# The near part added to the square table by VectorE, and the far and square products made by GpSimd

## The reference

```
x_aff = clip(x * a + b, -1.5, 1.5);  u = (x_aff + 1) * 0.5 * (K - 1)
i = floor(u);  t = clip(u - i, 0, 1);  b0..b3 = cubic basis of t
spline = alpha[i-1]*b0 + alpha[i]*b1 + alpha[i+1]*b2 + alpha[i+2]*b3     (indices clipped to 0..K-1)
y = id_gain * x + sum over r of spline[r] * mix[c, r] + bias
```

## Time and profile before

| what | value |
|---|---|
| time, median of 3 runs | 1149.39 us (1149.33 to 1150.38) |
| span of the profiled execution, first to last instruction | 1143.4 us |
| the rest, around the span | 6.0 us, if the profiled execution took the median time |
| busy share of PE / DVE / ACT / POOL | 95% / 85% / 79% / 12% |
| spline stage | from about 416 us to the end |

### The profile page before, as it was taken

How to read it: one execution, slowest core, us unless ns; L and a number is a source line. 1 busy time by engine, 2 the same in 40 slices (tenths; PEclk the granted TensorE clock), 3 DMA queues, 4 the chain that set the end, 5 groups by cost and what they waited for, 6 DMA issues and landing times.

```text
span 1143.4 us, 51639 instructions
## 1 busy us (share of the span) xinstructions
PE 1088.0 (95%) x23882; PEld 726.6 (64%) x23882; DVE 969.9 (85%) x959; ACT 898.8 (79%) x410; POOL 138.8 (12%) x195
## 2 busy tenths in 40 slices
PE   6999999699999959999999999999999999999996
PEld 5777777577777735666666656565665666566564
DVE  4856656687767679999999999999998999999997
ACT  4445453766777548999999999999999999999971
POOL 6000000068100000110101101011010110110100
PEclk9999999899999989999999999999999999999999
DMA  8677674677676937799999999989999989999652
GB/s 278 227 293 283 251 283 175 220 257 301 248 296 270 373 137 173 183 235 232 221 228 218 222 236 216 224 201 236 226 214 231 218 217 235 219 226 209 150 127 86
DMA packets 57459, 259.37 MB, mean 227 GB/s; under 512 B 16080, under 2 KB 16080, under 8 KB 49232
## 3 DMA queue, kind: packets, MB, share of 16 engines
q1 hardware_dynamic: 48496, 208.40, 56.0%
q0 software_dynamic: 8640, 48.17, 23.1%
q10 hardware_dynamic: 160, 0.30, 0.1%
HBM read 104.29 MB, written 77.07 MB: 159 GB/s over the span
## 4 chain that ended last, share of the span: by engine, by line
PE 86%; DVE 7%; issue 3%; DMA 1%; ACT 1%; SPq 0%; ACTq 0%; DVEq 0%
PE tab L1302 48%; PE acc L741 30%; PE tab L1311 7%; DMA halo<-y_scratch 1%; DMA w_raw<-in_w 1%; DVE middle_mask L1160 1%; ACT xin L381 1%; ACT yout L420 1%; DVE far L1187 0%; DVE far_sq L1209 0%; DVE stats L547 0%; DVE lin L1139 0%; DVE offset L1153 0%; DVE edge_mask L1169 0%; DVE poly L1215 0%
## 5 line engine op out<-in xcount | busy, mean ns | idle before, releaser
L1302 PE MATMUL tab<-edge_mask,diag 128*32 128x392 bf16 x10240 | 447.6, 329 | 6.1 <-issue 3.2
L1302 PEld LDWEIGHTS tab<-edge_mask,diag 128*32 128x32 f16 x10240 | 277.0, 97 | 171.0 <-issue 29.4
L1057 ACT ACTIVATE edge_mask<-cell,thr 128x6272 bf16<-128x6272 bf16 x62 | 338.6, 5508 | 1.7 <-DMA cell<-cell 1.7
L420 ACT ACTIVATE yout<-acc 128x1568 f32<-128x1568 f32 x64 | 94.5, 1477 | 167.2 <-PE acc L741 146.3
L741 PE MATMUL acc<-band_split,w 64*64 64x385 f16 (+2 forms) x4608 | 194.8, 329 | 9.8 <-DVE band_split L509 4.5
L741 PE MATMUL acc<-split,w 64*64 64x385 f16 (+3 forms) x4608 | 191.5, 326 | 11.5 <-DVE w L468 10.5
L547 DVE BATCH_NORM_STATS2 stats<-yout 128x392 f32 (+1 forms) x240 | 117.9, 555 | 88.8 <-ACT yout L420 88.8
L1302 PE MATMUL tab<-middle_mask,diag 128*32 128x392 bf16 x4096 | 185.1, 329 | 6.7 <-issue 4.5
L741 PEld LDWEIGHTS acc<-band_split,w 64*64 64x64 f16 x4608 | 148.3, 109 | 56.1 <-issue 8.8
L741 PEld LDWEIGHTS acc<-split,w 64*64 64x64 f16 x4608 | 144.8, 108 | 57.5 <-issue 12.2
L1302 PEld LDWEIGHTS tab<-middle_mask,diag 128*32 128x32 f16 x4096 | 109.2, 97 | 70.3 <-issue 7.7
(11 more groups left out here) (140 smaller groups left out, 961.6 us busy)
## 6 DMA issues: line engine op xcount, KB each, us to landing
y_scratch<-yout SPq DMA_DIRECT2D x32, 1568.0 KB, 6.1
cell<-cell SPq DMA_DIRECT2D x496, 98.0 KB, 5.1
xin<-y_scratch SPq DMA_DIRECT2D x16, 1568.0 KB, 6.2
lin<-far POOLq DMA_DIRECT2D x32, 784.0 KB, 9.4
out<-lin SPq DMA_DIRECT2D x31, 784.0 KB, 5.8
xin<-in_x SPq DMA_DIRECT2D x15, 1568.0 KB, 6.8
lin<-y_scratch SPq DMA_DIRECT2D x30, 784.0 KB, 9.3
lin<-in_x POOLq DMA_DIRECT2D x28, 784.0 KB, 8.1
```

Source lines behind the costliest of these rows:

```text
L420: act.activation(yout[b][:, :].rearrange("p (r k x) -> p k r x", r=2, k=TILES)[:, 2 * part:2 * part + 2], acc[:, 4 * part:4 * part + 4, 0: ...
L1057: act.activation(mask_of(c, q)[:, :, :], cell4[c % 2][:, :, :], ACT.Sign, bias=thr[:, q:q + 1]).then_inc(sign_mask_ready, 1)
L1302: mm = pe.matmul(tab[(c + t) % 2][j * GROUP:(j + 1) * GROUP, sub, 0:SUB], keep["diag"][part][:, j % 2, t, q, :], mask_of(c, q)[:, j, sub * ...
```

## The change

Five edits, all but one in `spline`:

1. PE no longer adds poly into the square table: `add_near_part` and its wait are gone. `square` on DVE now adds poly where it multiplied by `dist_sq`, and the result still has to be multiplied.
2. POOL makes that product (`square_term`), the product of far and its square (`far_part`, formerly on DVE, where it was also scaled by AMP), and the sum of both (`add_terms`), each one tensor_tensor on 128x1568 f32. `add_far`, the accumulating DMA, is gone.
3. On DVE `slope` writes over `offset`, `slope_and_far` takes the place of `add_slope` (it adds the slope to far), `value` adds to far, and `finish` waits for POOL's sum.
4. ACT makes three of the four blocks of the first edge mask; DVE makes the fourth (`edge_block`, 128x1568). PE's first use of that mask waits for both.
5. Waits follow the data: `distance`, `far_square` and `distance_square` on ACT wait for POOL's results. In the convolution stage one small reduction is cut in two, for the constant that belongs to the fourth block.

```
-            def add_near_part(c, sub):
-
-                return pe.matmul(tab[(c + T_SQ) % 2][:, sub, 0:SUB], keep["ident"][:, :],
-                                 poly[c % 2][:, sub * SUB:(sub + 1) * SUB], start=False, stop=True)
...
+            def far_part(c):
+                pool.wait_ge(table_used, used(c, T_FAR))
+                pool.wait_ge(far_sq_ready, c + 1)
+                pool.tensor_tensor(far[c % 2][:, :], far[c % 2][:, :], far_sq[:, :],
+                                   ALU.mult).then_inc(far_part_ready, 1)
...
+            def square_term(c):
+                pool.wait_ge(table_used, used(c, T_SQ))
+                pool.wait_ge(dist_sq_ready, c + 1)
+                pool.tensor_tensor(poly[c % 2][:, :], poly[c % 2][:, :], dist_sq[:, :],
+                                   ALU.mult).then_inc(square_ready, 1)
...
+            def add_terms(c):
+                pool.wait_ge(square_ready, c + 1)
+                pool.wait_ge(table_used, used(c, T_VAL))
+                pool.tensor_tensor(far[c % 2][:, :], far[c % 2][:, :], poly[c % 2][:, :],
+                                   ALU.add).then_inc(terms_added, 1)
...
+            def edge_block(c):
+                dve.wait_ge(copied[c % 2], copies(c))
+                wait_past(dve, table_ready, TABLES * (c - 1))
+                q = EDGE_QUADS[0]
+                dve.tensor_scalar(mask_of(c, q)[:, 3, :], cell4[c % 2][:, 3, :], keep["above"][:, q:q + 1], 2.0,
+                                  ALU.is_ge, ALU.mult).then_inc(edge_block_ready, 1)
...
             def square(c):
+                dve.wait_ge(table_used, used(c, T_NEAR))
                 dve.wait_ge(table_ready, used(c, T_SQ))
                 dve.scalar_tensor_tensor(out=quarters(poly[c % 2]), in0=summed(c, T_SQ), scalar=base(c, T_SQ),
-                                         in1=quarters(dist_sq), op0=ALU.add,
-                                         op1=ALU.mult).then_inc(table_used, 1)
+                                         in1=quarters(poly[c % 2]), op0=ALU.add,
+                                         op1=ALU.add).then_inc(table_used, 1)
...
+            def slope_and_far(c):
+                dve.wait_ge(table_used, used(c, T_LIN))
+                dve.wait_ge(far_part_ready, c + 1)
+                dve.scalar_tensor_tensor(out=far[c % 2][:, :], in0=sloped(c), scalar=1 / POINT,
+                                         in1=far[c % 2][:, :], op0=ALU.mult, op1=ALU.add).then_inc(slope_ready, 1)
...
             def finish(c):
-                dve.wait_ge(table_used, used(c, T_VAL))
-                dve.wait_ge(far_added, 16 * (c + 1))
-                dve.scalar_tensor_tensor(out=lin_of(c)[:, :], in0=poly[c % 2][:, :], scalar=cc(AMP),
+                dve.wait_ge(terms_added, c + 1)
+                dve.wait_ge(lin_ready, c + 1)
+                dve.scalar_tensor_tensor(out=lin_of(c)[:, :], in0=far[c % 2][:, :], scalar=cc(AMP),
                                          in1=lin_of(c)[:, :], op0=ALU.mult, op1=ALU.add).then_inc(whole, 1)
```

More of the change, by code:

```diff
@@ L606, in steps @@
                 signed = step[:, 0, :, 0:STEPS:2]
-                link(dve.tensor_reduce(halves[:, :], signed, AX.X, ALU.add), chain)
+                link(dve.tensor_reduce(halves[0:3 * GROUP, :], signed[0:3 * GROUP], AX.X, ALU.add), chain)
+                link(dve.tensor_reduce(halves[3 * GROUP:P, :], signed[3 * GROUP:P, :, STEPS // 4:STEPS // 2], AX.X,
+                                       ALU.add), chain)
                 link(dve.tensor_copy(keep["plain"][:, :], coef[:, 0, :, 0]), chain)
@@ L896, in used, with sloped @@
             return TABLES * c + t + 1
+        def sloped(c):
+            return offset[c % 2][:, :].bitcast(F32)
         def image_half(t, c):
@@ L976, in _ @@
                     add_x(c + 3)
-                add_far(c)
+                far_part(c)
+                square_term(c)
+                if c < CHUNKS - 1:
+                    add_terms(c)
         @block.scalar
@@ L1030, in distance @@
                 act.wait_ge(offset_ready, c + 1)
-                wait_past(act, whole, c - 1)
+                wait_past(act, terms_added, c - 1)
                 act.activation(poly[c % 2][:, :], offset[c % 2][:, :], ACT.Abs, scale=1 / POINT).then_inc(dist_ready, 1)
@@ L1036, in far_distance @@
                 act.wait_ge(dist_ready, c + 1)
-                wait_past(act, far_added, 16 * (c - 1))
+                wait_past(act, whole, c - 1)
                 act.activation(far[c % 2][:, :], poly[c % 2][:, :], ACT.Relu, bias=cc(MINUS_1)).then_inc(far_ready, 1)
@@ L1056, in edge @@
                 wait_past(act, table_ready, TABLES * (c - 1))
-                act.activation(mask_of(c, q)[:, :, :], cell4[c % 2][:, :, :], ACT.Sign,
+                blocks = slice(0, 3 if q == EDGE_QUADS[0] else 4)
+                act.activation(mask_of(c, q)[:, blocks, :], cell4[c % 2][:, blocks, :], ACT.Sign,
                                bias=thr[:, q:q + 1]).then_inc(sign_mask_ready, 1)
@@ L1208, in slope @@
[L1208 to L1216, removed]
+                dve.wait_ge(dist_ready, c + 1)
@@ new lines, in slope @@
+                dve.wait_ge(dist_sq_ready, c + 1)
+                dve.wait_ge(table_ready, used(c, T_LIN))
+                dve.scalar_tensor_tensor(out=quarters(sloped(c)), in0=summed(c, T_LIN), scalar=base(c, T_LIN),
+                                         in1=quarters(offset[c % 2]), op0=ALU.add, op1=ALU.mult).then_inc(table_used, 1)
+            def slope_and_far(c):
+                dve.wait_ge(table_used, used(c, T_LIN))
+                dve.wait_ge(far_part_ready, c + 1)
+                dve.scalar_tensor_tensor(out=far[c % 2][:, :], in0=sloped(c), scalar=1 / POINT,
+                                         in1=far[c % 2][:, :], op0=ALU.mult, op1=ALU.add).then_inc(slope_ready, 1)
@@ L1264, in _ @@
             linear(0)
-            far_part(0)
+            edge_block(1)
             middle(1, MIDDLE_QUADS[0])
@@ L1270, in _ @@
             middle(1, MIDDLE_QUADS[1])
-            add_slope(0)
+            slope_and_far(0)
             value(0)
@@ L1282, in _ @@
                 finish(c - 1)
+                if c + 1 < CHUNKS:
+                    edge_block(c + 1)
                 far_cube(c)
-                far_part(c)
                 if c + 1 < CHUNKS:
@@ L1292, in _ @@
                     middle(c + 1, MIDDLE_QUADS[1])
-                add_slope(c)
+                slope_and_far(c)
+            last_terms()
             closing_quarters()
@@ L1358, in table @@
                         mm = product(c, t, q, sub)
[L1359 to L1362, removed]
                 mm.then_inc(table_ready, 1)
```

39 lines of the change are left out of this document (20 added, 19 removed).

## The result

The changed kernel takes 1259.84 us (median of 4 runs, 1258.72 to 1260.22) against 1149.89 for the kernel before: ratio 1.0945, 95% interval 1.0915 to 1.0975. It is slower by 110 us, where 84 were forecast; the time is 27 us above the forecast 1233 and inside the range.

A forecast was written before the change was run, and what follows sets the result against it. PE bounded the kernel before; afterwards DVE's step, 19.6 us plus 5.0 of POOL stalls, would be 24.6 against 21.94. 30 steps add 80 us, chunk 0 to 1 adds 3, the tail 1: 1149.4 + 84 = 1233 us, range 1172 to 1300.

The forecast's parts named there:

- What the engines need: Spline stage, per chunk after the change: PE 18.69 us, ACT 20.0, DVE 19.6 before any stalls.
- POOL's instruction: Each of POOL's three tensor_tensors on 1568 f32 elements takes 3.5 us, the middle of 3.22 and 3.84.
- Mutual hold: DVE and POOL hold each other for whole instructions over shared SBUF ports; DVE instructions reading a table from PSUM are free.
- First and second stall: DVE's offsets, then the second middle mask, each start 1.67 us late per chunk because POOL's product holds them.
- Third stall: add_terms gets in only with near_cube, after fixed and linear, so finish waits 1.67 us for its result.
- Sum: DVE's 19.6 us plus 5.0 of stalls gives a 24.6 us step; 30 steps over 21.94 add 80 us.
- The head: The step from chunk 0 to 1 has the same instructions and adds 3 us.
- The tail's 1 us: From the last far_cube's start to DVE's end: some 17.5 us against 16.8 before, 1 us more.
- the 6.0 us around the span: Time outside the profiled span of 1143.4 us, added to make the starting time 1149.4 us.
- no wait for the cells at edge_block and none for x at position: edge_block's wait for the spread cells and add_x's later place in POOL's queue were both counted as nothing.
- What the removed DMA is worth: The accumulating DMA into lin goes; no wait of the chain hangs on it, so it was counted as nothing.
- PE at 75% of the stage: Sign in the profile after: PE busy some 75% of the spline stage, waiting for DVE.

The follow-up runs named there:

- v2_product_into_dist_sq: The version with two POOL products beside pairs of PSUM readers, changed so the square product is written over dist_sq and the accumulating DMA reads it there: 1430.9 us, ratio 1.2446.

## Why the prediction held, step by step

- **What the engines need.** PE 18.7, ACT 20.0, DVE 19.6 us per chunk were forecast. With the holds gone the step is 19.70 us with ACT never idle, and DVE's own time is 19.35. edge_block takes 0.62 us, forecast 0.56.
- **POOL's instruction.** 3.5 us from one row at 576 elements; measured 3.51 to 3.53. It is the middle of two bounds, 3.22 and 3.84, both wide of it; that it came out so near is luck. Forecast was also that the first and the third are lengthened; the second was too, by offsets (4.26 us).
- **Mutual hold.** The step on which all rested, inferred from rows in which only POOL waits. Shown now: DVE waits for the end of POOL's instruction, both the fast tensor_scalars and the STT with two inputs in SBUF. By the lock rule of the Trainium skill ("SBUF — State Buffer", "Who interferes with whom") it had to be so; the trace agrees, with offsets 2.54 for 0.97 us, and also in that the PSUM readers kept 1.84 us.
- **First and second stall.** Forecast 1.67 each, at offsets and at the second middle. Measured 1.57 and 1.51, at these places.
- **Third stall: the right instruction of POOL, the wrong place and size.** I let fixed and linear both pass before add_terms and forecast 1.67 us at finish. POOL got in between the two, linear was held for nearly the whole of POOL's instruction, 3.22 us, and finish hardly waited at all (2.2 us, two times). This step failed; I had taken from the earlier trace rows that POOL does not get in between two such instructions, and behind fixed it did, in every chunk. Its price is 1.55 us per chunk, and moving near_cube in between gave it back.
- **Sum.** Step 24.6 forecast, 25.45 measured, 30 x 0.85 = 25 us. The head grew by 9.1 us, not 3: edge_block was held once there, 3.88 us for 0.62, a middle mask once and linear once more; some 2 us of it lie before the spline stage, which runs of one kernel also scatter by, and stay unexplained. The tail's 1 us was 0.7 (the forecast's 16.8 us run to DVE's last instruction, at 1140.5, not to the span's end). Steps, head and tail together are 31 us above the forecast, the time only 27. The rest lies in the 6.0 us around the span that the forecast added: in every run whose span is on record the time is 1.7 to 1.9 us above it (1260.22 for 1258.4). If that holds for the kernel before too, its profiled execution took some 1145 us, 4 less than the median, and the forecast started 4 us too high for its span.
- **Nothing forecast, nothing found:** no wait for the cells at edge_block and none for x at position shows from 480 to 1240 us. What the removed DMA is worth was counted as nothing and not measured by itself. PE at 75% of the stage was forecast and is 226.47 of 300 us.

## What to carry to other kernels

Before work goes from VectorE to GpSimd, list what VectorE runs beside it: each instruction with two inputs in SBUF and each fast tensor_scalar waits for the end of the GpSimd instruction, and the moved work costs VectorE about its full length less what PSUM readers cover, here 6.3 us for work that VectorE does in 5.3. Put such an instruction where two PSUM readers stand side by side, and hold it back by a semaphore until they start; what replaces the third instruction, here a DMA, has its own price. And a held instruction looks busy: compare durations with free ones before reading busy shares.

## What the runs showed of the hardware

- A waiting POOL tensor_tensor got in between two DVE instructions that both hold it when the first took 0.62, 0.96 or 1.09 us; the second then took 4.3 us for 1.09, or 5.12 for 1.84. Behind a mask of 1.84 us it did not, in 29 chunks of 30, nor did a POOL tensor_scalar behind an STT of 1.8 us; but one that started together with such an STT did (288.39 us in `v2_product_into_dist_sq`). Scalars from SBUF or in the instruction make no difference (4.31 and 4.30 us). Whether the length of the first or the moment of POOL's start decides is open.
- Of two accumulating DMAs issued by POOL close together, 784 KB each, the second lands late whichever it is: 12.4 against 8.2 us with 3.4 us between the issues, and 13.9 against 8.0 with the order swapped and 0.6 us between. In the kernel before, with over 10 us between them, they took 9.4 and 8.1 us.
